# Conv-attention and recurrent block on one core: outputs over 64 rows into two banks, contexts divided in one instruction, a permuted residual by DMA, and a new order on every engine

## The reference

```python
x = x + conv(_gn(x))          # _gn: every channel over its 256 tokens
# conv: q, k, v = split(x @ w_qkv), 4 heads of 32; q = softmax(q over channels) * scale
#       k = softmax(k over tokens); context = k v^T; out = context^T q
#       out = layernorm(out @ w_out + b_out) * g_ln + b_ln
t = tokens(x)
t = t + attention(layernorm(t), Wq, Wk, Wv)      # causal, one head
t = t + rnn(layernorm(t), W, V, gamma, beta)
# rnn: Wx = batchnorm(t @ W.T) over all 16*256 rows; y_t = sigmoid(Wx_t + y_{t-1} @ V.T)
```

## Time and profile before

| | us |
|---|---|
| median of 3 runs (lowest, highest) | 112.45 (112.42, 113.61) |
| the profiled execution, its own time | 113.85 |
| its span (first to last instruction) | 112.0 |
| busy PE / DVE / ACT / POOL | 97.4 / 76.7 / 50.5 / 36.4 |

### The profile page before, as it was taken

One profiled execution on the slowest core, in us unless ns is written; L12 is line 12 of the kernel. 1 busy time (PEld: TensorE's weight loads), 2 busy tenths in 40 slices (PEclk: granted clock), 3 DMA queues, 4 the chain that ended last, 5 costly groups with the idle time before them and its releaser, 6 DMA issues.

```text
span 112.0 us, 2606 instructions
## 1 busy us (share of the span) xinstructions
PE 97.4 (87%) x982; PEld 71.9 (64%) x988; DVE 76.7 (68%) x226; ACT 50.5 (45%) x142; POOL 36.4 (32%) x66
## 2 busy tenths in 40 slices
PE   4977999998999997898999988999968797999930
PEld 1434485678767665676786756768844376999910
DVE  5989897766489899879989567467388659100080
ACT  4041155102414433774356894661825665666500
POOL 5626851000000849497046610404870020000020
PEclk9999999999999999999999999999999999999996
DMA  2641000000000000000000000000000000000006
GB/s 38 113 67 18 0 0 3 6 0 0 0 6 0 0 0 6 0 3 0 6 3 0 0 6 0 3 0 6 0 0 0 0 6 0 0 0 6 0 17 170
DMA packets 6284, 1.35 MB, mean 12 GB/s; under 512 B 5216, under 2 KB 6272, under 8 KB 6272
## 3 DMA queue, kind: packets, MB, share of 16 engines
q1 hardware_dynamic: 5728, 0.92, 4.9%
q10 hardware_dynamic: 544, 0.26, 0.8%
HBM read 0.66 MB, written 0.52 MB: 11 GB/s over the span
## 4 chain that ended last, share of the span: by engine, by line
PE 53%; DVE 30%; issue 5%; ACT 4%; POOL 4%; POOLq 0%
PE bank L1218 7%; PE pair L1561 6%; PE pair L1594 5%; PE bank L1191 4%; PE bank L1330 4%; PE pair L1157 4%; DVE ctxo L824 3%; PE pair L1294 3%; PE pair L1163 2%; DVE z L835 2%; DVE tc L857 2%; DVE ln_mean L852 2%; DVE ln_mean L853 2%; PE pair L1133 2%; DVE ln_sum L844 2%
## 5 line engine op out<-in xcount | busy, mean ns | idle before, releaser
L505 ACT ACTIVATE eqk<-pair 128x512 f32<-128x512 f32 x16 | 8.5, 601 | 13.6 <-PE pair L1176 13.6
L1218 PE MATMUL bank<-ctxo,eqk 128*128 128x132 f32 x64 | 11.0, 309 | 1.6 <-DVE ctxo L824 0.8
L405 POOL TENSOR_TENSOR z<-z 128x512 f32<-128x512 f32 x4 | 5.1, 1265 | 21.4 <-DVE z L835 21.3
L1561 PE MATMUL pair<-wxn,ident 128*128 128x124 f32 (+3 forms) x56 | 10.7, 276 | 0.7 <-DVE wxn L1020 0.7
L1218 PEld LDWEIGHTS bank<-ctxo,eqk 128*128 128x128 f32 x64 | 9.1, 207 | 3.2 <-issue 2.0
L545 ACT ACTIVATE eqk<-pair 128x384 f32<-128x384 f32 x16 | 7.0, 496 | 5.0 <-PE pair L1313 5.0
L1561 PEld LDWEIGHTS pair<-wxn,ident 128*128 128x128 f32 x56 | 8.4, 192 | 1.2 <-DVE wxn L1020 1.2
L1594 PE MATMUL pair<-warm,vT_bd 128*128 128x124 f32 (+3 forms) x44 | 8.5, 274 | 0.0
L1031 DVE TENSOR_TENSOR out_tok<-bank,eqk 128x384 f32<-128x384 f32 x2 | 1.1, 558 | 10.5 <-PE bank L1565 10.5
L694 ACT ACTIVATE warm<-pair 128x124 f32<-128x124 f32 (+2 forms) x20 | 5.5, 276 | 3.9 <-PE pair L1594 3.9
L835 DVE TENSOR_TENSOR z<-bank,qsum_r 128x256 f32<-128x256 f32 x16 | 6.8, 425 | 0.6
(11 more groups left out here) (198 smaller groups left out, 233.0 us busy)
## 6 DMA issues: line engine op xcount, KB each, us to landing
x_tok<-in_x_dram SPq DMA_DIRECT2D x8, 64.0 KB, 2.4
out_dram<-out_tok SPq DMA_DIRECT2D x2, 128.0 KB, 2.8
out_dram<-out_tok ACTq DMA_DIRECT2D x2, 128.0 KB, 3.2
w_raw<-in_L_conv_w_qkv_dram SPq DMA_DIRECT2D x1, 48.0 KB, 2.2
wout_sb<-in_L_conv_w_out_dram SPq DMA_DIRECT2D x1, 16.0 KB, 2.2
brow<-in_L_conv_b_out_dram SPq DMA_DIRECT2D x1, 16.0 KB, 3.2
gln_bc<-in_L_conv_g_ln_dram SPq DMA_DIRECT2D x1, 16.0 KB, 2.6
bln_bc<-in_L_conv_b_ln_dram SPq DMA_DIRECT2D x1, 16.0 KB, 3.0
```

The source lines that it names most:

```text
L505: act.activation(eqk[:, r, g], bank[g][:], ACT.Exp).then_inc(s_expA, 1)
L1218: ins = pe.matmul(bank[(7, 4)[g % 2]][:, h * 132:(h + 1) * 132], eqk[:, r, g, h * P:(h + 1) * P], ctxo[:, r % 2, g, :], start=True, stop=True)
L1561: pe.matmul(part(c, s)[:, :, j0:], ident[:], wxn[:, m, c * RPC:(c + 1) * RPC, j0 + at:CHUNKS + at], start=True, stop=False)
```

## The change

- `outs(r, i)` takes two images at once. The contraction is cut in two: `f` picks 64 of the 128 rows (two heads), with 66 columns instead of 132, and the halves go to two banks, 6 and 7, now one tensor `opair`. Eight matmuls for two images, where there were four.
- `ctxo` holds 66 columns for an image; its divide is one DVE instruction, and `contexts` on PE writes 130 columns for two images instead of 66. `heads(r, i)` on DVE divides two images with two instructions.
- `t2` goes to `resid` in permuted order by eight DMAs on SP; `rest` and the DVE copies are gone.
- `center` folds the scaling of the mean into the subtraction.
- The group norm's power on POOL is a logarithm and an exponential on ACT; `wqk4_b`, `xnT_b` of round 0, and the copies of `weights_5` go from DVE to ACT; the padding of `v1` goes from DVE to POOL; `tnT_b` goes from ACT to POOL. The clearing of `ctxo` goes away, that of `proj` grows from 264 to 520 columns.
- The work that used bank 6 uses bank 4, `wbank` alternates between 6 and 4.
- Every engine's list has a new order. PE has three fillers around `x_in(3)` where there was one, none ahead of `max_a(0, 0)` where there were two, none before `outs(0, 0)`, and eight behind the batch norm's matmul where there were two and the `rest` matmuls.

```diff
-        bank += [ctx.enter_context(nc.psum_tensor(f"bank{i}", [P, 512], F32)) for i in range(4, 8)]
+        bank += [ctx.enter_context(nc.psum_tensor(f"bank{i}", [P, 512], F32)) for i in range(4, 6)]
+        opair = ctx.enter_context(nc.psum_tensor("pair3", [P, 2, 512], F32))
+        bank += [opair[:, 0], opair[:, 1]]
...
+            return z4[:, r].rearrange("p k n -> p (k n)").rearrange("p (i f n) -> p i f n", i=2, f=2)
...
+            def residual_out(r):
...
+                for h in range(HALVES):
+                    at = (r % RPC) * CHUNKS + h * (CHUNKS // 2)
+                    sp.dma_start(resid[at:at + CHUNKS // 2, r // RPC].rearrange("j m g c -> j m (g c)"),
+                                 t2[:, r, h * G:(h + 1) * G].rearrange("p g c -> p (g c)")).then_inc(s_res[r // RPC], 16)
...
-            def gn(r):
-                pool.wait_ge(s_gnve, r + 1)
-                pool.tensor_tensor(gn_rs[:, r:r + 1], gn_ve[:, r:r + 1], halfneg[:, 0:1], ALU.pow).then_inc(s_gnrs, 1)
...
             def gn_cast(r):
                 pool.wait_ge(s_xnT, r + 1)
                 pool.tensor_copy(xnT_b[:, r], xnT[:, r]).then_inc(s_xnTb, 1)
...
+            def values_pad():
+                pool.memset(v1[:, :, :, :, C + 1:], 0.0)
+                pool.memset(v1[:, :, :, :, C:C + 1], 1.0).then_inc(s_pad, 1)
...
-                pool.wait_ge(s_z4, G * (r + 1))
-                link(pool.tensor_tensor(z4[:, r, :, 0:2 * C], z4[:, r, :, 0:2 * C], z4[:, r, :, 2 * C:4 * C], ALU.add))
-                pool.tensor_tensor(z[:, r], z4[:, r, :, 0:C], z4[:, r, :, C:2 * C], ALU.add).then_inc(s_z, 1)
+                pool.wait_ge(s_z4, 2 * (r + 1))
+                w = heads_of(r)
+                link(pool.tensor_tensor(w[:, :, 0], w[:, :, 0], w[:, :, 1], ALU.add))
+                w = w[:, :, 0].rearrange("p i (h a n) -> p i h a n", h=HALVES, a=2)
+                pool.tensor_tensor(z[:, r].rearrange("p (h i a) c -> p i h a c", h=HALVES, i=2),
+                                   w[:, :, :, :, 0:C], w[:, :, :, :, C:2 * C], ALU.add).then_inc(s_z, 1)
...
+            heads(0)
             gn_cast(3)
-            heads(0)
...
             residual_in(1)
-            residual_bias(3)
+            tnT_cast(0)
+            values_pad()
...
             residual_in(3)
+            tnT_cast(2)
             add_attention(0)
             center_2(0)
+            tnT_cast(3)
...
+            def gn(r):
...
+                act.activation(gn_log[:, r:r + 1], gn_mv[:, r, 1:2], ACT.Ln, bias=eps_c[:, 0:1]).then_inc(s_gnlog, 1)
+                act.wait_ge(s_gnlog, r + 1)
+                act.activation(gn_rs[:, r:r + 1], gn_log[:, r:r + 1], ACT.Exp, scale=-0.5).then_inc(s_gnrs, 1)
...
+            def weights_out():
...
+                act.activation(score_bd[:], bank[7][:, 0:P], ACT.Copy, scale=ATTN_SCALE)
+                act.copy(w3_bd[:], bank[7][:, P:4 * P]).then_inc(s_wts, 1)
...
-            def tnTb_out(r):
-                evac(tnT_b[:, r], tbank[r][:, 0:TW], s_T, r + 1, s_tnTb)
...
-            dve.memset(ctxo[:], 0.0)
...
-                link(dve.bn_aggr(gn_mv[:, r], gn_stats[:, r]))
-                dve.tensor_scalar(gn_ve[:, r:r + 1], gn_mv[:, r, 1:2], EPS, None, ALU.add).then_inc(s_gnve, 1)
+                dve.bn_aggr(gn_mv[:, r], gn_stats[:, r]).then_inc(s_gnve, 1)
...
-            def weights_5():
-                dve.wait_ge(s_wpe, 3)
-                dve.tensor_scalar(score_bd[:], bank[7][:, 0:P], ATTN_SCALE, None, ALU.mult)
-                dve.tensor_copy(wvT_bd[:], bank[7][:, P:2 * P])
-                dve.tensor_copy(wT_bd[:], bank[7][:, 2 * P:3 * P])
-                dve.tensor_copy(vT_bd[:], bank[7][:, 3 * P:4 * P]).then_inc(s_wev, 1)
-                dve.memset(v1[:, :, :, :, C + 1:], 0.0)
-                dve.memset(v1[:, :, :, :, C:C + 1], 1.0)
...
-                m = gbank[r][:, 256:256 + 2 * (2 * C + 2)].rearrange("p (b n) -> p b n", b=2)
+                m = gbank[r][:, 0:2 * (4 * C + 2)].rearrange("p (b n) -> p b n", b=2)
...
                 rk = ksum_r[:, r].rearrange("p (b a) -> p b a", b=2)
-                link(dve.reciprocal(rk, m[:, :, 2 * C:2 * C + 2]))
-                for e in range(HEADS):
-                    at = slice(C * e, C * (e + 1))
-                    ins = dve.tensor_tensor(ctxo[at, r % 2, :, at].rearrange("p (b a) c -> p b a c", b=2),
-                                            m[at, :, 0:2 * C].rearrange("p b (a c) -> p b a c", a=2),
-                                            rk[at, :, :, None].broadcast_to([C, 2, 2, C]), ALU.mult)
-                ins.then_inc(s_ctxS, 1)
...
-            def heads(r, g):
...
-                o = bank[(7, 4)[g % 2]][:, 0:264].rearrange("p (h n) -> p h n", h=2)
-                rq = qsum_r[:, r, g].rearrange("p (h e) -> p h e", h=2)
-                link(dve.reciprocal(rq, o[:, :, P:P + HEADS]))
-                dve.tensor_tensor(z4[:, r].rearrange("p (h g) (e c) -> p g h e c", h=2, e=HEADS)[:, g],
-                                  o[:, :, 0:P].rearrange("p h (e c) -> p h e c", e=HEADS),
-                                  rq[:, :, :, None].broadcast_to([P, 2, HEADS, C]), ALU.mult).then_inc(s_z4, 1)
+                link(dve.reciprocal(rk, m[:, :, 4 * C:4 * C + 2]))
+                dve.tensor_tensor(ctxo[:, r % 2, :, 0:2 * C].rearrange("p (b a) n -> p b a n", b=2),
+                                  m[:, :, 0:4 * C].rearrange("p b (a n) -> p b a n", a=2),
+                                  rk[:, :, :, None].broadcast_to([P, 2, 2, 2 * C]), ALU.mult).then_inc(s_ctxS, 1)
...
+            def heads(r, i):
...
+                dve.wait_ge(s_out, 2 * r + i + 1)
+                o = opair[:, :, 0:4 * (2 * C + 2)].rearrange("p f (k n) -> p f k n", k=4)
+                rq = qsum_r[:, r].rearrange("p g n -> p (g n)").rearrange("p (i f k s) -> p i f k s", i=2, f=2, k=4)[:, i]
+                link(dve.reciprocal(rq, o[:, :, :, 2 * C:2 * C + 2]))
+                dve.tensor_tensor(heads_of(r)[:, i].rearrange("p f (k s c) -> p f k s c", k=4, s=2),
+                                  o[:, :, :, 0:2 * C].rearrange("p f k (s c) -> p f k s c", s=2),
+                                  rq[:, :, :, :, None].broadcast_to([P, 2, 4, 2, C]), ALU.mult).then_inc(s_z4, 1)
...
             def center(n, src, r, done):
-                link(mean(n, src, r))
-                dve.tensor_tensor(tc[:, n - 1, r], src[:, r], bc(ln_mean[:, n, r]), ALU.subtract).then_inc(done, 1)
+                link(dve.tensor_reduce(ln_mean[:, n, r], src[:, r], AX_X, ALU.add))
+                dve.scalar_tensor_tensor(out=tc[:, n - 1, r], in0=bc(ln_mean[:, n, r]), scalar=-1.0 / C, in1=src[:, r],
+                                         op0=ALU.mult, op1=ALU.add).then_inc(done, 1)
...
             attend(2)
+            add_attention(2)
+            gain_2(2)
             attend(3)
-            add_attention(2)
             add_attention(3)
-            gain_2(2)
             gain_2(3)
...
-            for c in range(CHAINS):
-                dve.wait_ge(s_res, RPC * (c + 1))
-                link(dve.tensor_copy(resid[:, c].rearrange("p m g c -> p (m g c)"), rbank[c][:]))
...
-                n = 2 * C + 2
+                    pe.wait_ge(s_brow, 1)
+                n = 4 * C + 2
...
-                        ins = pe.matmul(gbank[r][C * e:C * (e + 1), 256 + n * b:256 + n * (b + 1)], gram[:, r, b, C * e:C * (e + 1)],
+                        ins = pe.matmul(gbank[r][C * e:C * (e + 1), n * b:n * (b + 1)], gram[:, r, b, C * e:C * (e + 1)],
...
-            def outs(r, g):
+            def outs(r, i):
...
-                if r == R - 1 and g == 1:
+                if r == 0 and i == 0:
...
+                    pe.wait_ge(s_xn1, 3)
+                else:
+                    pe.wait_ge(s_z4, 2 * r + i)
...
-                for h in range(HALVES):
-                    ins = pe.matmul(bank[(7, 4)[g % 2]][:, h * 132:(h + 1) * 132], eqk[:, r, g, h * P:(h + 1) * P],
-                                    ctxo[:, r % 2, g, :], start=True, stop=True)
+                n = 2 * C + 2
+                for a in range(2):
+                    for h in range(HALVES):
+                        for f in range(2):
+                            at = slice(2 * C * f, 2 * C * (f + 1))
+                            ins = pe.matmul(opair[:, f, n * (2 * h + a):n * (2 * h + a + 1)],
+                                            eqk[at, r, 2 * i + a, h * P:(h + 1) * P], ctxo[at, r % 2, 2 * i + a, :],
+                                            start=True, stop=True)
...
-                        at = (r % RPC) * CHUNKS + h * (CHUNKS // 2)
-                        ins = pe.matmul(rbank[r // RPC][at:at + CHUNKS // 2, m * P:(m + 1) * P], perm[:, m, :],
-                                        t2[:, r, h * G:(h + 1) * G].rearrange("p g c -> p (g c)"), start=True, stop=True)
-                if STRIDE - 1 in ms:
-                    ins.then_inc(s_res, 1)
...
             values(3, 0)
+            values_back(2)
             values(3, 1)
```

(19 more changed lines are left out.)

## The result

The changed kernel takes 102.53 us median (102.33 to 102.54), the kernel before 112.88 beside it (112.42 to 113.61): ratio 0.907, 95% interval 0.900 to 0.915. The forecast was 106.35 with a range from 102.0 to 110.5. The time lies in the range, but it is the time of rival 1, the clock that rises earlier (102.4, chance 0.20).

What follows compares the result with a forecast made beforehand. PE was taken to bound B and C2, PE and DVE nearly full in C1, D a chain of small steps. Terms -0.6 + 0 + 0 - 3.6 - 0.7 - 1.2 = -6.1 took 112.45 to 106.35 us, range 102.0 to 110.5.

Steps and rivals of the forecast that it cites:

- rival 1: PE's clock rises at the end of the setup, shortening the next stage: another -4 us, 102.4; chance 0.20.
- B: Round 0 and start of round 1, 16.1 to 31.4 us, bound by PE: 0, bounds +1.0 and -1.0.
- A: Setup to 16.1 us: DVE's clearing goes, `keys` no longer behind the shift; -0.6, bounds 0 and -1.0.
- `outs` on PE: Two images as eight half-row matmuls still take 1.07 us: 0, bounds over 7 pairs -2.4 and +2.7.
- C1: Rest of linear attention with first softmax rounds, 31.4 to 62.0 us: DVE savings give -3.6, bounds 0 and -6.2.
- C2: Rest of the attention, 62 to 82 us, bound by PE: mainly two fillers go; -0.7, bounds 0 and -1.5.
- the divide: `contexts` on DVE in C1, four instructions become one: -0.72 us in each of three rounds, -2.2.
- The scaling of the mean: DVE in C1, scaling folded into the subtraction: first two of three are on the chain, -1.4.
- D: Second layer norm and batch norm, 82 to 93.3 us: new order -1.8, later values +0.6; -1.2, bounds -0.2 and -2.4.
- E: Recurrence and store: 0; the eight fillers take 1.8 us, about the wait that they fill.
- Gain lost to PE (2): C1 gains nothing because PE is already full; A, C2 and D give half: 111.3 us; chance 0.12.
- One pair of banks (4): Each `outs` waits for `heads` to empty both banks; 1.2 us stall for each of seven, 114.8 us; chance 0.10.

Runs made afterwards that it cites:

- b_fill: Kernel before with three more fillers in the setup, nothing else changed: 108.47 us, ratio 0.96; looked at again for a trace, 108.44 us.
- a_nofill: Changed kernel without its three fillers around `x_in(3)`: 102.81 us, ratio 0.908; two other executions took 119.9, one of them the traced one.
- a_neg: Changed kernel with the old order around `neg_a(0)` on PE and `shift_a(0)` behind `gn_apply(2)` on DVE: 102.66 us.
- a_wdve: Changed kernel with the four copies of the prepared weights and the padding of `v1` back on DVE: 102.78 us.
- a_tail: Changed kernel with the second layer norm's old order put back on DVE, PE and ACT: 103.41 us, ratio 0.9143.
- a_center: Changed kernel with the centring in three instructions again (sum, scaling, subtraction) in place of two: 102.9 us, ratio 0.9066.
- a_outs_f: Changed kernel with each `outs` doing all lower-row matmuls, then all upper: `outs` 1.61 us against 1.11; executions took 114.66 to 133.6 us at reduced granted clocks.
- a_endfill: Changed kernel with two fillers behind the batch norm's matmul in place of eight: 105.37 us, ratio 0.9259.

## Why the prediction was right, and where it was not

**The clock.** I read rightly that PE ran at 1.2 GHz until 31.4, and priced an earlier rise at -4 and 102.4. Measured: -4.5 by the ratio (b_fill) and 102.53. What failed is the weight: I gave the unchanged rise 0.44 and the early one 0.20, on the ground that B before was as dense. b_fill shows how little it took in the kernel before: three fillers in the setup. What brings it in the changed kernel is not known, since it comes without its three fillers too (a_nofill). The range holds only because I had stretched it to take in this rival; by the forecast's own story the time would have been 106.35.

**A, -0.6: too small. B, 0: right within its bounds.** At the same clock the last `shifts_a(0)` comes 1.64 us earlier. From there to the last `shifts_a(1)` it takes 8.54 us for 7.84, but 1.11 of these are an `outs` that stood behind it: -0.41. Together -2.05, for -0.6 forecast. At the low level A gained 2.3, past my bound of -1.0, and B nothing (a_nofill). In A I costed DVE's clearing and gave part of it back to ACT. That part was about right: DVE ends `max_a(0)` at 10.74 where it ended at 11.59. I did not cost that `neg_a(0)` now stands ahead of the queries and `shift_a(0)` ahead of `gn_apply(2)`: `shift_a(0)` ran at 13.79 on DVE and runs at 11.74, so the shifts no longer wait for it. The total hardly hangs on it (a_neg). In B, at the high level, the old chain is DVE's, so what left DVE counts, though for 0.4 us (a_wdve) and not for the 2 that I had named.

**`outs` on PE, 0: right, for another reason.** The pair takes 1.11 us; I said 1.07. But I held the range from 0.73 to 1.46 to be a question of whether halves overlap, and took a value between. Now both effects are apart: splitting alone makes it 1.61, past my bound, the overlap takes 0.50 back, and they nearly cancel. The Trainium skill's page "TensorEngine Tiling (Array Packing)", section "Theoretical Speedup", allows up to 2x for a contraction of 64: here the alternation gives 1.61 / 1.11 = 1.45, and against the unsplit matmuls nothing. The rule of the Trainium skill's page "TensorE: Matmul & The Clock Gate", Part 2, that a load's time goes by columns and not by rows, agrees with this trace: a load of 64 rows takes 188 ns at the median, one of 128 rows 190.

**C1, -3.6, and C2, -0.7: too large.** At the same clock, from the last `shifts_a(1)` to the last `values_back(3)`, the kernel gained 3.16, of which 1.11 is the `outs` done earlier: -2.05 for -4.3 forecast. By terms: the divide -2.2, measured -1.95. The scaling of the mean -1.4, measured -0.1: the step that failed. DVE does save 1.6 us in four rounds, but I took the chain of the kernel before as the chain of the changed one, where the steps behind the centring wait for PE or ACT. I also took a row of 1.01 us for the price of an instruction that costs 0.17; of such a delay by POOL a part stays with the fused instruction. `heads` -0.6 and the longer `contexts` +0.6 (0.65 for 0.40, so +0.25 a round) stay unmeasured alone; the sum leaves about nothing for them and for C2. `max_b` does not wait for POOL's cast: round 1's starts at 49.46, 2.2 us after the cast ended.

**D, -1.2: too small in sum, right in its mechanism.** From `values_back(3)` to the last `normalize` it takes 4.02 us for 5.97 at the same clock: -1.95, of which 0.2 comes back behind it. The order is worth 1.1 (a_tail), the fused centring 0.2 (a_center); the remaining 0.65 was not tried. The traces of DVE have 0.30 of it in the two additions of `t1` (1.17 us in b_fill_look, 0.87 in a_tail) and 0.27 in a wait for ACT ahead of the last `normalize`. My +0.6 for the later values is in C2's distance, and was 0.2 (a_tail).

**E, 0: right as a sum, wrong as a reason.** The stage takes 18.65 us for 18.70. I costed the eight fillers by the time they take. They take none, and without six of them the stage takes 2.8 us more. In the kernel before, two fillers and the `rest` matmuls stood at that point; that these had kept the level up is likely and was not tried.

**The sum.** -0.6 +0 -4.3 -1.2 = -6.1 was forecast for the edits, and -2.05 -2.05 -1.76 = -5.9 is measured at equal clock. It agrees because A and D were short by what C was over. That is luck, and should not be taken as a confirmation of the terms.

**The other rivals.** Gain lost to PE (2): not all of it, but C1 and C2 gave half of their 4.3, with PE busy for 26.77 of C1's 29.93 us. One pair of banks (4): the wait is there, 0.66 and 0.16 us before two of the seven `outs` in C1, not 1.2 before each. DVE reaches `heads` in time.

**What I said would show it.** DVE's busy time fell by 12.1 (10 to 13 said). Of the three `contexts` divides in C1 two left the chain and one stays, at 34.68; none ends an idle time of PE of more than 0.3. The fillers did not change near 31.

## What to carry to other kernels

Before pricing a change in DVE or ACT work, find from two equal instructions when PE's clock rises, and ask what the change does to PE's idle time ahead of that point and ahead of every chain of short matmuls: here three fillers were worth 4.5 us at the start of the kernel before, and six were worth 2.8 at the end of the changed one, about as much as the best single edit. A step on the chain of the old kernel is priced by what waits for it in the new one: where other edits have moved the chain to PE, 1.6 us saved on DVE were worth 0.1. And a row that is long because of a neighbour's work is no price of its instruction. Splitting a contraction pays only as far as neighbouring matmuls alternate between the parts of the array, and it first has to earn back the doubled number of loads.

## What the runs showed of the hardware that was unexpected

- The same eight 64-row matmuls of 66 columns, 0.50 us apart (1.11 and 1.61) by the order of issue alone.
- The level of PE's clock can fall in the middle of dense work: in a_outs_f from 31.6 to 52.1 us, with PE busy for 5.46 of the 6.57 us before the fall and for 20.01 of the 20.48 us behind it. No run tells why.
- PE at the low level costs a chain of small dependent matmuls nearly double, more than the rows of its matmuls show (0.64 for 0.39 us): the first 24 records of the recurrence take 5.28 us in a_endfill and 2.78 in the changed kernel.
- On DVE, a scaling of 8 elements takes 0.17 us alone. Where POOL is at work it ends 0.02 to 0.03 us after POOL's instruction, or after the second of two in a row, and takes 0.39 to 1.01 (five rows, of before and a_center). The fused 256-element instruction takes 0.43 beside POOL's clearing at 38.34, and 0.82 and 0.89 beside its additions.
